# Three edits between the second feed-forward net and linear attention: gate products, weight loads, and the hand-over of the channel copies

## The chip, the cores and the metric
The kernel runs on one core of a Trainium2 chip. The metric is the device time of one execution, in microseconds (us); lower is better. The five engines named here are TensorE (PE, matrix products and transpositions; PEld is its weight load), VectorE (DVE), ScalarE (ACT), GpSimd (POOL) and SyncE (SP, which here only issues DMAs). Each works through its own queue in order, and they meet at semaphores.

## The reference, cut to what matters
A two-layer decoder over 4 batches of 512 tokens with 256 channels (2,048 tokens, 16 tiles of 128). Six blocks follow one another, each closed by a layer norm over channels:

```python
x = _layernorm(x + L0_attn(x))             # a recurrence with decay, 16 heads
x = _layernorm(x + L0_xattn(x, ctx))       # ternary weights, 8-bit activations, ends in a feed-forward net
x = _layernorm(x + L0_ffn(x))              # 8 experts, top 2 for each token
x = _layernorm(x + L1_attn(x))             # linear attention
x = _layernorm(x + L1_xattn(x, ctx))       # cross-attention to 1601 keys
x = _layernorm(x + L1_ffn(x))              # two layers of windowed attention and gelu net
```

The change touches the end of the second block, the third, and the start of the fourth. The experts' block takes scores `x @ Wg` (256 by 8), picks two experts for each token, sends the normalised token through `relu(h @ W1 + b1) @ W2 + b2` of each, and adds both, weighted, to the token. Linear attention begins with `q` and `kv` products of the token's 256 channels with a 256 by 768 matrix, `phi(x) = elu(x) + 1` on q and k.

## The kernel before, in words
Tokens are held twice: `x_tok` with tokens on the partitions (norms, sums) and `x_ch` with channels on the partitions (right operand or left operand of the next products). A group is the four tiles of one batch. The step from `x_tok` to `x_ch` is a *turn* of a group: eight transpositions on TensorE (`turn_pe`, L237) into two PSUM banks, then a copy of one half by ScalarE (L1520) and of the other by VectorE (L1490).

**End of the second block** (`bitnet_ffn_pe`, L1382 on). An output loop over 16 tiles makes 8 products for each (L1408); VectorE adds them to `x_tok` (L1473), and after each four tiles takes the norm of the group (L209 to L217). After tiles 7, 11 and 15 TensorE turns groups 0, 1 and 2. Behind the loop stand the gate products (`gate_pe`, L1433: products of `x_ch` with the 256 by 8 gate matrix) of groups 0, 1 and 2, then the turn of group 3, then the gate products of group 3. A `settle` lets every engine wait for the last copies of group 3. VectorE begins the experts with statistics of all 16 tiles (L1732), then reads the scores.

**Experts** (`experts_*`). SP loads the weights of experts 0, 1 and 2 (two DMAs of 1 MB each, L1630 and L1631), stores the normalised tokens `hats` to DRAM (L1639), then loads experts 3 to 7, with the bias matrix `b2` (L1644) after expert 4. VectorE and TensorE work out which 256 token rows go to which of 23 slots. GpSimd gathers the rows of a slot from `hats` with two indirect DMAs (L1995), slots 0 and 1 ahead of all else, the others as their buffers come free. For each slot TensorE transposes the rows (L1688), makes four groups of first products (L1704) and, one slot later, the second products (L1717). VectorE adds `b2` (L1890), GpSimd scatters the rows (L2012). When all slots are through, SP reads the pairs back, VectorE combines them group by group (L1898), and each group is normed by ScalarE (L1973, which waits for a reciprocal and a mean of VectorE, L1919 and L1921) and turned by TensorE. ScalarE's order is: norm of group g, then copy of group g - 1. VectorE's is: combine group g, finish the norm scale of g - 1, copy group g - 2.

**Start of linear attention** (`linear_*`). A `settle` makes all engines but SP wait for the last copies of group 3; SP waits for them too after it has issued the loads of `wqkv` and `wproj`. TensorE then makes the q and kv products of batch 0 (L2186 two steps, L2193 four steps), of batch 1, and so on, each step into the next of banks 4 to 7. For a q step VectorE takes the minimum (L2255), ScalarE makes relu and exp, VectorE adds (L2257).

Of the kernel before, what the change touches and what calls it, by code (L numbers as in the profile page):

```python
# [14 lines left out]
B, T, D = 4, 512, 256  # L15
NTOK = B * T
TILES = NTOK // P
# [321 lines left out]

def settle(m, last, but=None):  # L340

    nc = m.nc
    for e in (nc.tensor, nc.vector, nc.scalar, nc.gpsimd, nc.sync):
        if e is but:
            continue
        for wait in last:
            e.wait_ge(*wait)
# [1033 lines left out]
def bitnet_ffn_pe(m, s, t, use):  # L1381
# [20 lines left out]
    for tile in range(TILES):  # L1402
# [7 lines left out]
        if tile % 4 == 3 and tile > 4:  # L1410
            g = tile // 4 - 1
            pe.wait_ge(*s.normed(TPB * g + TPB))
            for h in range(HALVES):
                turn_pe(m, use["channels", g, h], m.x_tok, g, h)
    for g in range(B - 1):
        gate_pe(m, s, t, use, g)
    pe.wait_ge(*s.normed(TILES))
# [136 lines left out]
def experts(m, gate, split):  # L1554
    nc = m.nc
    with ExitStack() as ctx:
# [39 lines left out]
        steps = [("place",), ("inverse",)] + [p for p in plan if p[0] in ("turn", "first", "second")]  # L1596
        steps += [("channels", g, h) for g in range(B) for h in range(HALVES)]
        use = m.banks(steps, tuple(range(8)))
        use["gate",] = gate
        experts_sp(m, s, moved, t, use, plan, split)  # L1600
        experts_pe(m, s, moved, t, use, plan)
        experts_dve(m, s, moved, t, use, plan)
        experts_act(m, s, t, use, plan)
        experts_pool(m, s, moved, t, use)
        over = [use["channels", B - 1, h].done for h in range(HALVES)]
        settle(m, over, but=nc.sync)
    return use["second", SLOTS - 1].full, over

# [5 lines left out]
def x_loaded(moved, j):  # L1614
    return (moved.x0_loaded, moved.x1_loaded)[j % 2]
# [10 lines left out]
def experts_sp(m, s, moved, t, use, plan, split):  # L1626
# [10 lines left out]
    for tile in range(0, TILES, 4):  # L1637
        sp.wait_ge(*s.hat_made(tile + 4))
        sp.dma_start(hats[:, tile:tile + 4, :], t["hat"][:, tile:tile + 4, :]).then_inc(*s.stored.up(16))  # L1639
    for e in range(3, NE):  # L1640
        weights(e)
        if e == 4:
            sp.wait_ge(*s.stored(16 * TILES // 4))
            sp.dma_start(t["b2"], dram["moe_b2"].unsqueeze(0).to_broadcast([P, NE, D])).then_inc(*s.b_loaded.up(16))  # L1644
# [9 lines left out]
def experts_pe(m, s, moved, t, use, plan):  # L1654
# [24 lines left out]
    for step in plan:  # L1679
# [27 lines left out]
        elif kind == "second":  # L1707
# [11 lines left out]
            ins.then_inc(*u.fill)  # L1719
    for g in range(B):  # L1720
        pe.wait_ge(*s.normed(TPB * g + TPB))
        for h in range(HALVES):
            turn_pe(m, use["channels", g, h], m.x_tok, g, h)


# [346 lines left out]

def linear_attention(m, kept, weights_free, over):
    nc = m.nc
    with ExitStack() as ctx:
# [12 lines left out]
                      "low raised phi v_copied scaled closed joined xw_loaded ctx_loaded k_stored0 k_stored1 w_high w_low c_split a_low b_low "  # L2088
                      "in_high v_ones x_high x_low q_high q_stored")
        plan = linear_plan()  # L2090
# [8 lines left out]
        use.update(m.banks([p for p in plan if p[0] in ("keys", "value", "queries")], (0, 2)))  # L2099
        linear_sp(m, s, t, use, plan, weights_free, over)  # L2100
        linear_pe(m, s, t, use, plan, nth)
        linear_dve(m, s, t, use, plan, nth)
        linear_act(m, s, t, use, plan, nth)
        linear_pool(m, s, t, plan, use)
        settle(m, [use["channels", B - 1, h].done for h in range(HALVES)] + [use["value", AHEAD - 1, KT - 1].done]
# [66 lines left out]

def linear_pe(m, s, t, use, plan, nth):
    pe = m.nc.tensor
    wqkv = t["wqkv"]
    loaded = (s.rg0_loaded, s.rg1_loaded, s.rg2_loaded, s.rg3_loaded)
    pe.wait_ge(*s.w_loaded(32))
    for step in plan:
        kind, b = step[:2] if len(step) > 1 else (step[0], None)
        if kind in PREPARED:  # L2180
            prepare_pe(m, s, t, use, step, 0)
        elif kind == "q":
            c, u = step[2], use[step]
            pe.wait_ge(*u.empty)
            for h in range(HALVES):
# [196 lines left out]

def linear_pool(m, s, t, plan, use):
    g = m.nc.gpsimd
    for n in range(AHEAD):
        g.memset(t["v"][n][:, :, :, NX:VC], 1.0).then_inc(*s.v_ones.up())
    g.wait_ge(*s.v_ones.now())
    for step in plan:
        kind, b = step[:2] if len(step) > 1 else (step[0], None)
        if kind == "parts":  # L2390
            g.wait_ge(*s.closed.now())
            g.wait_ge(*s.x_low.now())
            context_pool(m, s, t, b)
        elif kind == "x_split":
            split_pool(m, s, t, use, b)
        elif kind == "scale":
            g.wait_ge(*s.scaled(b + 1))
            g.tensor_tensor(projected(m, b), projected(m, b), over_tiles(m, "la_beta"), ALU.add).then_inc(*s.closed.up())
# [1201 lines left out]
def build(nc, dram):  # L3600
# [8 lines left out]
    with ExitStack() as ctx:  # L3609
# [7 lines left out]
        with ExitStack() as first:  # L3617
# [7 lines left out]
            gate, split = bitnet(m, early)  # L3625
        weights_free, over = experts(m, gate, split)
        with ExitStack() as both:
# [4 lines left out]
                        c_high=[kb("xa_c_high%d" % n, [P, S2 + 1]) for n in range(2)], c_both=[kb("xa_c_both%d" % n, [P, S2 + 1]) for n in range(2)])  # L3632
            linear_attention(m, kept, weights_free, over)
            cross_attention(m, kept)
# [61 lines left out]
```

## Time and profile before
| | us |
|---|---|
| three runs, median (lowest to highest) | 2683.3 (2679.48 to 2683.9) |
| the profiled execution, its own time | 2684.69 |
| its span | 2683.4 |
| TensorE busy in the span | 2180.8 (81%) |
| VectorE busy | 1690.6 (63%) |
| ScalarE busy | 1192.3 (44%) |
| GpSimd busy | 593.5 (22%) |

Engine busy times overlap, so they don't add up. The mean granted TensorE clock is 0.902 of 2.4 GHz. A row of the timeline gives the start in us, the time it covers, the engine, the line, the operation with its output and inputs, how many were merged, and in brackets the idle time of the engine before them and who ended it.

### The profile page before, as it was taken

Reading aid. Unit: us, or ns where it says so; the run is one execution under the profiler, and the core shown is the slowest. Engines: PE = TensorE matmul, PEld = TensorE weight load, DVE = VectorE, ACT = ScalarE, POOL = GpSimd, SP = SyncE. Lnnn points to the kernel's source line nnn. Section 1 sums busy time; section 2 is a strip of 40 time slices with the busy share of each in tenths; the row PEclk is TensorE's granted clock in tenths of the full one; section 3 lists DMA queues with packets and bytes.
Section 4 is the critical chain, followed back from the end, with each engine's and each line's share of the span. In section 5 each row is a group of like instructions: output and inputs, shape, how many; then the busy total and the mean of one; then the engine's idle time right before and its main releaser. Section 6 shows DMA issues by size and latency. Waiting matters only on the chain. (4 is left out here: it accounts for less than half of the span.)

```text
span 2683.4 us, 42293 instructions
## 1 busy us (share of the span) xinstructions
PE 2180.8 (81%) x15608; PEld 1421.8 (53%) x15678; DVE 1690.6 (63%) x3439; ACT 1192.3 (44%) x2208; POOL 593.5 (22%) x529
## 2 busy tenths in 40 slices
PE   5996689897659995877799999967887786888677
PEld 3554157575449994443255555543555443555444
DVE  4875965466866665666666666616776533777663
ACT  2123855454333332423155555545665433666442
POOL 2110013133036661012100000003221322222142
PEclk8997789898779996888799999987999897999899
DMA  4111024343071112332311111020000001000100
GB/s 140 47 47 47 0 64 143 125 126 95 34 289 49 49 51 99 93 82 81 81 26 38 26 25 38 14 93 2 1 1 1 11 1 62 1 1 1 43 9 24
DMA packets 98936, 144.74 MB, mean 54 GB/s; under 512 B 25052, under 2 KB 78768, under 8 KB 96176
## 3 DMA queue, kind: packets, MB, share of 16 engines
q1 hardware_dynamic: 94320, 129.97, 15.7%
q0 software_dynamic: 4416, 12.06, 1.5%
q8 instruction: 131, 2.15, 0.4%
q14 instruction: 69, 0.57, 0.1%
HBM read 102.08 MB, written 39.85 MB: 53 GB/s over the span
## 5 line engine op out<-in xcount | busy, mean ns | idle before, releaser
L2795 DVE TENSOR_REDUCE xa_max<-psum 128x1 f32<-128x1024 f32 (+1 forms) x256 | 248.5, 988 | 132.1 <-PE psum L2705 131.5
L2876 ACT ACTIVATE xa_work<-psum 128x1024 f32<-128x1024 f32 (+1 forms) x208 | 212.7, 1024 | 188.1 <-PE psum L2728 186.1
L2743 PE MATMUL psum<-xa_work,xa_values 128*33 128x128 f32 (+1 forms) x3328 | 224.0, 277 | 0.0
L2743 PEld LDWEIGHTS psum<-xa_work,xa_values 128*33 128x33 f32 (+1 forms) x3328 | 168.2, 111 | 73.7 <-issue 70.2
L3066 PE MATMUL psum<-wqkv_l,x_hl_l 128*128 128x512 bf16 x538 | 138.5, 404 | 65.7 <-POOL x_hl_l L3326 32.9
L3432 PE MATMUL psum<-h_ch_f,w_f 128*128 128x512 bf16 (+1 forms) x556 | 135.0, 397 | 34.3 <-issue 13.1
L995 POOL TENSOR_TENSOR text_q<-text_q 128x512 bf16<-128x512 f32 x64 | 80.7, 1275 | 345.9 <-ACT text_q L1365 345.7
L2728 PE MATMUL psum<-xa_query_rows,xa_key_rows 98*128 98x512 bf16 (+1 forms) x416 | 127.3, 388 | 8.4 <-ACT xa_work L2876 7.7
L1704 PE MATMUL psum<-moe_rows,moe_w 128*128 128x256 bf16 x1104 | 129.7, 275 | 5.0 <-issue 5.0
L2705 PE MATMUL psum<-xa_key_rows,xa_query_rows 96*128 96x512 bf16 (+1 forms) x512 | 126.6, 344 | 8.4 <-ACT xa_work L2876 3.7
L1960 ACT CAST x_ch<-moe_raw 128x512 bf16<-128x512 f32 x92 | 56.9, 618 | 158.3 <-DVE moe_raw L1875 157.7
L3066 PEld LDWEIGHTS psum<-wqkv_l,x_hl_l 128*128 128x128 bf16 x576 | 56.4, 103 | 132.0 <-issue 50.6
L1717 PE MATMUL psum<-moe_w,x_ch 128*128 x1104 | 124.1, 273 | 0.0
L3300 ACT ACTIVATE w_p_l<-psum,w_max_l 128x256 f32<-128x256 f32 (+1 forms) x256 | 110.4, 457 | 28.8 <-DVE w_max_l L3204 28.7
L1704 PEld LDWEIGHTS psum<-moe_rows,moe_w 128*128 x1104 | 108.8, 99 | 18.7 <-issue 5.6
L3432 PEld LDWEIGHTS psum<-h_ch_f,w_f 128*128 128x128 bf16 (+1 forms) x576 | 56.4, 102 | 110.2 <-issue 32.0
L1717 PEld LDWEIGHTS psum<-moe_w,x_ch 128*128 128x128 bf16 x1104 | 108.0, 98 | 12.5
L1236 PE MATMUL psum<-ctx_f,query_sum 128*128 128x512 f32 (+1 forms) x256 | 105.0, 536 | 7.9 <-DVE query_sum L1288 7.9
L3337 POOL TENSOR_TENSOR qk_other_l<-qk_raw_l,rotary_l 128x256 f32<-128x256 f32 x64 | 64.6, 1010 | 195.2 <-DVE qk_rot_l L3188 195.2
L1257 PE MATMUL psum<-ctx_f,probs_t_bn 128*128 128x128 f32 (+1 forms) x832 | 100.0, 277 | 2.8 <-DVE probs_t_bn L1314 2.7
L1358 ACT ACTIVATE probs_bn<-psum,softmax_bn 128x1024 f32<-128x1024 f32 x64 | 58.8, 924 | 90.7 <-DVE softmax_bn L1305 90.7
L1257 PEld LDWEIGHTS psum<-ctx_f,probs_t_bn 128*128 128x128 f32 (+1 forms) x832 | 95.4, 192 | 3.5 <-DVE probs_t_bn L1314 3.4
(474 smaller groups left out, 4851.0 us busy)
## 6 DMA issues: line engine op xcount, KB each, us to landing
text_q<-in_moe_w SPq DMA_DIRECT2D x64, 256.0 KB, 3.8
experts<-text_q SPq DMA_DIRECT2D x64, 256.0 KB, 3.0
moe_w<-experts SPq DMA_DIRECT2D x16, 1024.0 KB, 10.0
xa_key_rows<-cross_keys SPq DMA_DIRECT2D x48, 200.1 KB, 3.5
ctx_chunk<-in_ctxT SPq DMA_DIRECT2D x24, 300.0 KB, 3.1
cross_keys<-xa_k_hl SPq DMA_DIRECT2D x6, 800.5 KB, 3.8
moe_w<-pairs_out SPq DMA_DIRECT2D x8, 512.0 KB, 6.8
xa_ctx_f<-in_ctxT SPq DMA_DIRECT2D x4, 800.5 KB, 4.8
```

The costliest lines, as they stand in the source:

```text
L1236: ins = pe.matmul(u.wide[:, c0 - a:c1 - a], t["qsum"][:, n * P:(n + 1) * P], t["keys"][:, b * S2 + c0:b * S2 + c1], start=True, stop=True)
L1257: ins = pe.matmul(u.ap[:, 0:P], t["turned"][n % 2][0:rows, kt, :], t["values"][0:rows, n // TPB, kt, :], start=(kt == 0), stop=(kt == KT - 1))
L1704: ins = pe.matmul(u.ap[:, a * SLOT:(a + 1) * SLOT], w1[:, w, h, cf], t["x"][j % 2][:, x, h, :], start=(h, k) == (0, 0), stop=(h, k) == (1, 2))
L1717: ins = pe.matmul(u.ap[:, a * D:(a + 1) * D], t["hidden"][j % 2][:, x, f, q], w2[:, w, f, :], start=(f, k) == (0, 0), stop=(f, k) == (7, 2))
L2705: ins = pe.matmul(u.wide[:, x - c0:y - c0], t["q_rows"][n % 3][0:SPLIT, a, qt * P:(qt + 1) * P], t["k_rows"][n % 3][0:SPLIT, a, x:y], star ...
L2728: ins = pe.matmul(u.wide[0:rows, a * T:(a + 1) * T], t["k_rows"][n % 3][:, a, kt * P:kt * P + rows], t["q_rows"][n % 3][:, a, :], start=Tr ...
L2743: ins = pe.matmul(total.ap[a * LANE:a * LANE + VC, c:c + PIECE], t["v"][b][0:rows, kt, first + a, :], exps[0:rows, a, c:c + PIECE], start= ...
L2795: v.tensor_reduce(t["maxes"][n % 2][:, qt * HU + a, part:part + 1], u.wide[:, 0:c1 - c0], AX.X, ALU.max).then_inc(*u.free)
L2876: act.activation(t["exps"][k % EXPS][0:rows], u.wide[0:rows].rearrange("p (m q) -> p m q", q=T), ACT.Exp, scale=1.0 / float(np.sqrt(np.flo ...
L3066: ins = pe.matmul(b.ap, x[:, i, h, w * P:(w + 1) * P], t["wqkv"][:, j, h, cols], start=(h, n) == (0, 0), stop=(h, n) == (1, 2))
L3300: ins = act.activation(t["p"][n % 2][:, i, lo:2 * P], scores[:, i, :], ACT.Exp, bias=t["peak"][n % 2][:, i:i + 1], scale=8.0, accum_out=t[ ...
L3432: ins = pe.matmul(u.ap[0:rows, :], t["w1"][:, y, h, o:o + rows], t["h_ch"][g % 2][:, x, h, :], start=(h, n) == (0, 0), stop=(h, n) == (1, 2))
```

## The change
Three edits:

1. In the output loop of the second block, the gate products of group g - 1 follow the turn of group g (for g = 1 and 2). Behind the loop only the gate products of group 2 stand ahead of the turn of group 3.
2. SP waits until both gathers of slot 0 have landed before it loads experts 3 to 7. `b2` follows expert 3 rather than expert 4, and its own wait for the stored `hats` goes.
3. The `settle` between experts and linear attention goes. The turns of the four groups are a function that linear attention calls on TensorE: group 0 first, then the wait for `wqkv`, the first four steps of the plan (q, q, kv, kv of batch 0), then the turns of groups 1, 2 and 3, then the rest of the plan. Each q step waits for the copies of its batch. GpSimd and SP wait for the copies of group 3 as before; ScalarE and VectorE go on after their own last copy. The turns use banks 0 to 3; linear attention has semaphores of its own.

```diff
@@ bitnet_ffn_pe
             for h in range(HALVES):
                 turn_pe(m, use["channels", g, h], m.x_tok, g, h)
-    for g in range(B - 1):
-        gate_pe(m, s, t, use, g)
+            if g:
+                gate_pe(m, s, t, use, g - 1)
+    gate_pe(m, s, t, use, B - 2)
@@ experts
-        steps += [("channels", g, h) for g in range(B) for h in range(HALVES)]
         use = m.banks(steps, tuple(range(8)))
+        use.update(m.banks([("channels", g, h) for g in range(B) for h in range(HALVES)], tuple(range(4))))
-        experts_pe(m, s, moved, t, use, plan)
+        turn = experts_pe(m, s, moved, t, use, plan)
...
-        over = [use["channels", B - 1, h].done for h in range(HALVES)]
-        settle(m, over, but=nc.sync)
@@ experts_sp
+    sp.wait_ge(*x_loaded(moved, 0)(32))
     for e in range(3, NE):
         weights(e)
-        if e == 4:
-            sp.wait_ge(*s.stored(16 * TILES // 4))
+        if e == 3:
             sp.dma_start(t["b2"], ...)
@@ experts_pe
-    for g in range(B):
+    def turn(g):
         pe.wait_ge(*s.normed(TPB * g + TPB))
         for h in range(HALVES):
             turn_pe(m, use["channels", g, h], m.x_tok, g, h)
+    return turn
@@ linear_pe
+    turn(0)
     pe.wait_ge(*s.w_loaded(32))
-    for step in plan:
+    for n, step in enumerate(plan):
+        if n == 4:
+            for g in range(1, B):
+                turn(g)
...
         elif kind == "q":
+            for wait in channels[b]:
+                pe.wait_ge(*wait)
@@ linear_pool
+    for wait in over:
+        g.wait_ge(*wait)
```

## Rows read from the trace of the kernel before
**Rows 1.** Timeline, end of the second block: start, us covered, engine, line, operation.
```profile
714.04 3.66 PE L1408 MATMUL psum<-bn_q_f,hidden_q 128*128 128x256 bf16 x32
...
718.53 1.66 DVE L1473 SCALAR_TENSOR_TENSOR x_tok<-psum,out_scale,x_tok 128x256 f32<-128x256 f32 x4
719.16 1.06 PE L237 MATMUL psum<-const,x_tok 128*128 128x128 f32 x8 [1.46 <-DVE x_tok L1473]
...
720.06 8.29 PE L1433 MATMUL psum<-moe_wg,x_ch 128*128 128x8 f32 x48
...
723.25 1.38 DVE L217 TENSOR_SCALAR x_tok<-x_tok,ln_mean_var,ln_rstd 128x256 f32<-128x256 f32 x4
...
728.20 1.95 PE L237 MATMUL psum<-const,x_tok 128*128 128x128 f32 x8
...
730.19 0.69 DVE L1490 COPY x_ch<-psum 128x512 f32<-128x512 f32 x1 [5.55 <-PE psum L237]
...
731.03 3.55 PE L1433 MATMUL psum<-moe_wg,x_ch 128*128 128x8 f32 x16 [0.88 <-DVE x_ch L1490]
...
731.13 5.26 DVE L1732 BATCH_NORM_STATS2 ln_stats<-x_tok 128x6 f32<-128x256 f32 x16
```
**Rows 2.** Windows: us, busy (instructions) by engine, granted clock, DMA share, GB/s.
```profile
720.00:722.00 2.00, 2.00 (x22) 2.00 (x19) 1.93 (x6) 0.41 (x1) 0.00 (x0) 1.00 0.00 0
...
722.00:723.00 1.00, 1.00 (x8) 1.00 (x7) 0.64 (x5) 0.29 (x1) 0.00 (x0) 0.60 0.00 0
```
**Rows 3.** Timeline, the gathers of slots 0 and 2 and the first bias addition.
```profile
762.27 0.99 POOL L1995 DMA_INDIRECT moe_rows<-hats,come_from  x1 [0.30 <-issue]
...
768.71 1.12 PE L1688 MATMUL psum<-const,moe_rows 128*128 128x128 f32 x4 [9.20 <-DMA moe_rows<-hats,come_from]
...
780.15 0.95 POOL L1995 DMA_INDIRECT moe_rows<-hats,come_from  x1 [0.30 <-issue]
...
786.11 0.66 PE L1688 MATMUL psum<-const,moe_rows 128*128 128x128 f32 x4 [0.84 <-DMA moe_rows<-hats,come_from]
...
795.43 0.69 DVE L1890 TENSOR_TENSOR moe_rows<-psum,moe_rows 128x512 f32<-128x512 f32 x1
```
**Rows 4.** Line L1995 alone: issue to landing of all 46 gathers.
```profile
DMA to landing us min/median/max: 2.7/3.0/7.2
```
**Rows 5.** Waits in the experts' stretch: us in total, times, longest.
```profile
PEld psum L1688 <- DMA moe_rows<-hats,come_from: 10.5, 2, 9.4
```
**Rows 6.** Windows of the experts' start; last three numbers: clock, DMA share, GB/s.
```profile
764.00:766.00 2.00, 0.00 (x0) 0.00 (x0) 0.00 (x0) 0.00 (x0) 1.46 (x2) 0.50 1.01 414
...
793.00:800.00 7.00, 7.00 (x66) 6.32 (x65) 4.03 (x9) 2.68 (x5) 3.14 (x3) 1.00 0.12 41
```
**Rows 7.** Timeline, last norms of the experts and start of linear attention.
```profile
1056.89 0.56 ACT L1520 COPY x_ch<-psum 128x512 f32<-128x512 f32 x1
...
1064.10 2.07 ACT L1973 ACTIVATE x_tok<-x_tok,minus_mean,ln_rstd 128x256 f32<-128x256 f32 x4 [0.44 <-DVE minus_mean L1921]
...
1066.22 1.97 PE L237 MATMUL psum<-const,x_tok 128*128 128x128 f32 x8 [1.21 <-ACT x_tok L1973]
...
1068.23 0.69 DVE L1490 COPY x_ch<-psum 128x512 f32<-128x512 f32 x1 [2.49 <-PE psum L237]
...
1069.02 6.03 PE L2186 MATMUL psum<-x_ch,la_wqkv 128*128 128x512 f32 x8 [0.83 <-issue]
...
1072.81 0.75 DVE L2255 TENSOR_SCALAR la_min<-psum,cols 128x512 f32<-128x512 f32 x1 [3.65 <-PE psum L2186]
...
1074.89 7.03 PE L2193 MATMUL psum<-la_wqkv,x_ch 128*128 128x512 f32 x16
...
1079.57 0.68 DVE L2264 TENSOR_TENSOR la_kv<-psum,rows 128x512 f32<-128x512 f32 x1
...
1081.41 0.68 DVE L2264 TENSOR_TENSOR la_kv<-psum,rows 128x512 f32<-128x512 f32 x1
```
**Rows 8.** Windows, the clock at the start of linear attention (columns as in rows 2).
```profile
1073.00:1074.00 1.00, 1.00 (x2) 0.34 (x1) 0.56 (x1) 0.32 (x1) 0.00 (x0) 0.61 0.38 93
```

More of the change, by code:

```diff
@@ L337, in rwkv, with settle @@
         settle(m, last)
-def settle(m, last, but=None):
+def settle(m, last):
     nc = m.nc
     for e in (nc.tensor, nc.vector, nc.scalar, nc.gpsimd, nc.sync):
-        if e is but:
-            continue
         for wait in last:
@@ L1604, in experts @@
         experts_pool(m, s, moved, t, use)
-        over = [use["channels", B - 1, h].done for h in range(HALVES)]
-        settle(m, over, but=nc.sync)
-    return use["second", SLOTS - 1].full, over
+    return use["second", SLOTS - 1].full, turn, [[use["channels", g, h].done for h in range(HALVES)] for g in range(B)]
 def loaded(s, e):
@@ L2070, in value_steps, with linear_attention @@
     return [("value", b, kt) for kt in range(0, KT, 2)]
-def linear_attention(m, kept, weights_free, over):
+def linear_attention(m, kept, weights_free, turn, channels):
     nc = m.nc
@@ L2088, in linear_attention @@
                       "low raised phi v_copied scaled closed joined xw_loaded ctx_loaded k_stored0 k_stored1 w_high w_low c_split a_low b_low "
-                      "in_high v_ones x_high x_low q_high q_stored")
+                      "in_high v_ones x_high x_low q_high q_stored", first=80)
         plan = linear_plan()
@@ L2099, in linear_attention @@
         use.update(m.banks([p for p in plan if p[0] in ("keys", "value", "queries")], (0, 2)))
-        linear_sp(m, s, t, use, plan, weights_free, over)
-        linear_pe(m, s, t, use, plan, nth)
+        linear_sp(m, s, t, use, plan, weights_free, channels[B - 1])
+        linear_pe(m, s, t, use, plan, nth, turn, channels)
         linear_dve(m, s, t, use, plan, nth)
         linear_act(m, s, t, use, plan, nth)
-        linear_pool(m, s, t, plan, use)
+        linear_pool(m, s, t, plan, use, channels[B - 1])
         settle(m, [use["channels", B - 1, h].done for h in range(HALVES)] + [use["value", AHEAD - 1, KT - 1].done]
@@ L2170, in rows_sp, with linear_pe @@
     sp.dma_start(dram["cross_keys"][b].rearrange("x (o p) s -> o p x s", p=P)[o], t["k_hl"][o]).then_inc(*keys_stored(s, o).up(16))
-def linear_pe(m, s, t, use, plan, nth):
+def linear_pe(m, s, t, use, plan, nth, turn, channels):
     pe = m.nc.tensor
@@ L2380, in linear_act, with linear_pool @@
             bitnet_channels_act(m, use, b)
-def linear_pool(m, s, t, plan, use):
+def linear_pool(m, s, t, plan, use, over):
     g = m.nc.gpsimd
+    for wait in over:
+        g.wait_ge(*wait)
     for n in range(AHEAD):
@@ L3625, in build @@
             gate, split = bitnet(m, early)
-        weights_free, over = experts(m, gate, split)
+        weights_free, turn, channels = experts(m, gate, split)
         with ExitStack() as both:
@@ L3632, in build @@
                         c_high=[kb("xa_c_high%d" % n, [P, S2 + 1]) for n in range(2)], c_both=[kb("xa_c_both%d" % n, [P, S2 + 1]) for n in range(2)])
-            linear_attention(m, kept, weights_free, over)
+            linear_attention(m, kept, weights_free, turn, channels)
             cross_attention(m, kept)
```

## The prediction, made before the change was run
> **What bounds the kernel now.** I read the page first. Its first part has TensorE busy 81% of the span (the table above), but the three edits touch three short stretches in which it waits or works on something that nobody needs yet, so the share of the whole says nothing. I went on with the timeline of each stretch, asking each time which wait ends last, and with the windows for the granted clock and the DMA share.
>
> *End of the second block.* VectorE ends the norm of group 3 at 723.25 + 1.38 = 724.63, but TensorE turns the group only at 728.20, because 48 gate products stand in its queue until 728.35 [rows 1]. VectorE copies the turned half at 730.19 and starts the experts' statistics at 731.13. These end at 736.39; the last gate products end at 734.58, under them [rows 1]. So the statistics set the pace, and they hang on the turn.
>
> *Start of the experts.* TensorE waits 9.2 us for the gather of slot 0, issued at 762.27 and used at 768.71: 6.4 us, where the median of 46 gathers is 3.0 [rows 3, 4]. The DMA engines are full then (share 1.01), and nearly idle at 793 to 800, where TensorE is busy without a gap at full clock (share 0.12, busy 7.00 of 7.00) [rows 6]. Only one later gather is waited for [rows 5]: that of slot 2, issued 780.15, used 786.11, also about 6 us [rows 3]. What is saved ahead of slot 0 is thus kept to the end of the experts.
>
> *Start of linear attention.* After its last copy (1068.23 to 1068.92) VectorE stands idle 3.65 us until the first q product is there at 1072.81; TensorE starts at 1069.02 at half clock, and reaches 2.4 GHz at 1073.8 (0.61 in the window from 1073) [rows 7, 8]. From then on VectorE and ScalarE pass q and kv to and fro and TensorE is ahead.
>
> **Edit 1, gate products into the loop.** Nothing is added or removed: 48 products of 8 columns before, 16 + 16 + 16 after. At full clock 22 instructions fill 2.00 us [rows 2], so 16 cost 1.45 us. The 16 of group 0 now stand ahead of tiles 12 to 15, which take 3.66 us and end at 717.7; they would end at 719.2 [rows 1]. VectorE takes the four tiles from 718.53 at 0.41 us each, so it asks for the last at 719.8, and is not held up. The turn of group 2 starts at 719.25 for 719.16, 0.1 us late, and VectorE's chain with it: its norm of group 3 ends at 724.7. Meanwhile TensorE makes the gate products of group 1 (from 720.4) and 2 (to 723.4, if the clock holds; to about 724 if it falls at 722.6 as it does before, window 722 to 723 at 0.60 [rows 2]). Either way it is free, and turns group 3 at about 724.9 instead of 728.20. Price: **-3.3 us**. The last products are covered by the statistics with 736.39 - 734.58 = 1.8 us to spare. Bounds: if this turn also ran at full clock it would take 1.06 instead of 1.95 us [rows 1], so -4.2. At worst the clock falls while the gate products of group 0 run in the loop: these then take 2.9 us, the four tiles about 5.2 (half clock until the clock is back), the turn of group 2 starts at 722.3 and takes 1.95, and from its end VectorE needs the same 4.4 us (719.16 + 1.06 to 724.63) to the norm's end, 728.7: **+0.6**. I take the first: before, the clock fell 2.5 us into the gate products (720.06 to 722.6), and in the loop they last 1.45 us and output products follow at once.
>
> **Edit 2, weights held.** SP's ten loads of 1 MB and `b2` move behind the landing of slot 0's gathers. With idle queues I give the gather the median, 3.0 us: 762.27 + 3.0 = 765.3 for 768.71, **-3.4 us**. That the whole wait behind is engine work (transposition, cast, first products) makes it pass on. Queued behind SP's new wait: experts 3 to 7 and `b2`. At 414 GB/s [rows 6] these 11.5 MB take 28 us, 765 to 793. `b2`, third in the new order, has landed by some 773 and is first used at 795.43 - 3.4 = 792 [rows 3], so nearly 20 us are spare; expert 3, ahead of it in the queue, is used later still, in the fourth of 23 slots. The gather of slot 2 falls in the same crowd as before and I leave it its 6 us. Bounds: **0** if the first gather is slow for a reason of its own; if the gather of slot 2 comes with it, up to 0.84 us more [rows 3], -4.2; if that one takes the longest 7.2 us [rows 4] instead of 6.0, 1.2 is given back.
>
> Beside this the Trainium skill has a rule that speaks against the size of this term. "DMA: Bandwidth & Descriptors", section "Queues, rings and completion order", says that each DMA engine goes round between the queues that have work, one packet at a time, so a gather would not sit behind the backlog of the weights' queue but share with it. By that rule 256 KB beside a stream of 414 GB/s would lose about 0.6 us, an estimate, and not 3.4. The trace doesn't side with it: the two gathers that had a full stream beside them took twice the median. By the row the edit is worth 3.4, by the rule 0.6.
>
> **Edit 3, no stop.** The gain to be had is VectorE's 3.65 us of idling [rows 7]. But the turns of groups 1 to 3 now stand behind 16 fp32 products, and ScalarE copies group 1 before it norms group 3. On the clock of the trace before: copies of group 0 are done at 1056.89 + 0.56 = 1057.45, products start at 1057.5. At 1.2 GHz one takes 0.88, at 2.4 GHz 0.44 (7.03 / 16) [rows 7]. If the clock again rises 4.8 us after the first product (1069.02 to 1073.8 [rows 7, 8]), 5.5 are done by 1062.3 and the other 10.5 take 4.6: the turn of group 1 starts at 1066.9. At full clock it takes 1.06. VectorE copies group 1 from 1068.0 to 1068.7, then makes reciprocal and mean, for which ScalarE waits 0.44; the norm of group 3 starts at 1069.1 and takes 2.07 [rows 7]; the turn of group 3 starts at 1071.25; VectorE's last copy runs 1072.35 to 1073.04; the first q step of VectorE starts at about 1073.3, for 1072.81. Price: **+0.5 us**, and TensorE's head start hides nothing more, since VectorE doesn't wait for it after the first q step. The loads that SP issues behind the last copy come some 4 us later; they are first read only when VectorE is through batch 1. Bounds: if nothing is late but the products, the whole **-3.65**; if the clock stays at 1.2 GHz, 16 products take 14.1, turns 1.97, and VectorE starts at about 1079.8: **+7.0**.
>
> **Sum.** -3.3 - 3.4 + 0.5 = -6.2 us. Against the profiled execution's own 2684.69 us that is 2678.5. This execution lies 1.4 us over the median of the runs shown, 2683.3, so the median after should be 2683.3 - 6.2 = **2677.1**. No change is what lies within 0.2% (5.4 us) of the median, about what a measurement of this kernel can tell. The forecast stands just beyond that.
>
> **Rivals.**
> *The stop was worth its idle time* (edit 3 gives -3.65). For it: the 3.65 us are there. Against: group 3's norm waits behind ScalarE's copy of group 1, and that behind 16 products. Time: 2683.3 - 3.3 - 3.4 - 3.6 = 2673.0. Chance 0.12.
> *The first gather is slow by itself* (edit 2 gives 0): it is the first one after `hats` was written. Against: the gather of slot 2 was slow too. Time: 2683.3 - 3.3 + 0.5 = 2680.5. Chance 0.15. (The rule of the Trainium skill above, of "DMA: Bandwidth & Descriptors", would give near it, 2679.9.)
> *The clock falls inside the output loop* (edit 1 gives +0.6). For it: 8-column products now stand right behind a turn for which TensorE had idled, as they did where it fell. Time: 2683.3 + 0.6 - 3.4 + 0.5 = 2681.0. Chance 0.13.
> *Slower: TensorE stays at 1.2 GHz from 1057 to the end of batch 1's products.* It starts cold, is fed in pieces and is stopped three times by turns. Edit 3 then costs 7.0, and the kv steps of batch 1 come at 3.5 us each on TensorE while VectorE takes one in 1.84 (1079.57 to 1081.41 [rows 7]): over four steps at 1.7 us each, less the 2 us that TensorE is ahead, some 5 us more. Sum -6.7 + 12 = +5.3: 2688.6. It decides from the point where edit 3 costs over 6.7, which is where the turn of group 1 starts later than about 1071. Against: with 16 products in a row the clock rose after 4.8 us before. Chance 0.10.
>
> **How the numbers follow.** The forecast has 0.50. Its own scatter of some 2 us puts 0.31 of it beyond 5.4 us and 0.19 within. Faster: 0.31 + 0.12 + 0.02 = 0.45. Same: 0.19 + 0.15 + 0.11 less what scatters out = 0.42. Slower: the last rival and the scatter of the middle ones, 0.13. The range goes from 2672, the bound of the full gain of edit 3 and a little, to 2686, which takes in the middle rivals and the first 7 us of the slow one, and leaves out most of its rest.
>
> **What would show it.** Edit 1: the turn of group 3 within 0.5 us behind VectorE's norm of it, and tiles 12 to 15 read by VectorE without a gap. Edit 2: under 4 us from the issue of slot 0's second gather to TensorE's first transposition, with a DMA share near 0 in between. Edit 3: 16 products between the turns of groups 0 and 1; VectorE's first q step straight behind its last copy, its wait for the product gone; the time from ScalarE's copy of group 0 to that step 0.5 us longer than the 15.9 before (1056.89 to 1072.81 [rows 7]). I would be wrong if that stretch were shorter by over 2 us, if the gather stayed at 6, or if later stages, which the edits don't touch, moved by more than the sum.

## The result, and the profile after

The changed kernel takes 2671.21 us (median of 19 runs, 2666.8 to 2683.06), the kernel before beside it 2683.62 us (19 runs, 2679.48 to 2700.02). The ratio is 0.995, with a 95% interval from 0.9938 to 0.9962: 12.4 us faster, where I had forecast 6.2 and given a range that ended at 2672.0.

The page of the changed kernel, first part: busy time, share and instructions of each engine.
```profile
span 2681.7 us, 42368 instructions
...
PE 2188.0 (82%) x15678; PEld 1415.9 (53%) x15678; DVE 1691.5 (63%) x3439; ACT 1191.9 (44%) x2208; POOL 594.3 (22%) x529
```
Nothing was taken away; each engine is busy for the same time as before, to 0.5%. The execution that was profiled took 2683.06 us, the longest of the 19. Its first half is usual, its second half is not, so I read the second half from another profile of the same kernel (its own time 2671.95 us, below under "The changed kernel again").

**Edit 1.** Timeline of the changed kernel at the end of the second block; it answers to [rows 1]. Columns: start, us covered, engine, line, operation, idle before and releaser.
```profile
711.16 1.06 PE L237 MATMUL psum<-const,x_tok 128*128 128x128 f32 x8 [1.46 <-DVE x_tok L1472]
712.06 2.83 PE L1432 MATMUL psum<-moe_wg,x_ch 128*128 128x8 f32 x16
714.75 5.97 PE L1406 MATMUL psum<-bn_q_f,hidden_q 128*128 128x256 bf16 x32
...
718.36 0.48 DVE L1472 SCALAR_TENSOR_TENSOR x_tok<-psum,out_scale,x_tok 128x256 f32<-128x256 f32 x1 [1.22 <-PE psum L1406]
719.88 0.48 DVE L1472 SCALAR_TENSOR_TENSOR x_tok<-psum,out_scale,x_tok 128x256 f32<-128x256 f32 x1 [1.04 <-PE psum L1406]
720.56 1.04 PE L237 MATMUL psum<-const,x_tok 128*128 128x128 f32 x8
721.43 3.64 PE L1432 MATMUL psum<-moe_wg,x_ch 128*128 128x8 f32 x32
...
724.63 1.38 DVE L217 TENSOR_SCALAR x_tok<-x_tok,ln_mean_var,ln_rstd 128x256 f32<-128x256 f32 x4
726.06 1.73 PE L237 MATMUL psum<-const,x_tok 128*128 128x128 f32 x8 [0.99 <-DVE x_tok L217]
...
728.77 5.26 DVE L1732 BATCH_NORM_STATS2 ln_stats<-x_tok 128x6 f32<-128x256 f32 x16
```
The same kernel in windows: us, busy (instructions) of PE, PEld, DVE, ACT, POOL, granted clock, DMA share, GB/s.
```profile
712.06:713.00 0.94, 0.94 (x10) 0.94 (x9) 0.87 (x3) 0.35 (x1) 0.00 (x0) 0.84 0.00 0
713.00:714.75 1.75, 1.75 (x10) 1.75 (x11) 1.65 (x8) 0.03 (x1) 0.00 (x0) 0.50 0.00 0
714.75:717.00 2.25, 2.25 (x12) 1.61 (x13) 1.90 (x6) 0.26 (x1) 0.00 (x0) 0.50 0.00 0
717.00:720.50 3.50, 3.50 (x23) 2.64 (x21) 1.10 (x3) 0.00 (x0) 0.00 (x0) 0.64 0.00 0
```
The turn of group 3 starts 726.06 - 726.01 = 0.05 us behind VectorE's norm of it, as meant, and 3.6 us after the norm in the kernel before [rows 1]. But the clock falls to half, 1.2 GHz, during the gate products of group 0 and is still there in tiles 12 to 15: 16 gate products take 2.83 us and not 1.45, the four tiles 5.97 and not 3.66, VectorE stands waiting between the tiles, and the turn of group 2 comes 720.56 - 711.16 = 9.40 us after that of group 1, before 719.16 - 713.13 = 6.03. From the turn of group 1 to the statistics it is 17.61 us, before 18.00: **-0.4 us**.

**Edit 2.** Timeline of the changed kernel, the gathers of slots 0 and 2; it answers to [rows 3].
```profile
760.06 0.99 POOL L1995 DMA_INDIRECT moe_rows<-hats,come_from  x1 [0.30 <-issue]
762.91 1.11 PE L1685 MATMUL psum<-const,moe_rows 128*128 128x128 f32 x4 [5.66 <-DMA moe_rows<-hats,come_from]
774.35 0.95 POOL L1995 DMA_INDIRECT moe_rows<-hats,come_from  x1 [0.30 <-issue]
780.60 0.66 PE L1685 MATMUL psum<-const,moe_rows 128*128 128x128 f32 x4 [1.13 <-DMA moe_rows<-hats,come_from]
```
The window between the first two of them, columns as above.
```profile
760.06:762.91 2.85, 0.00 (x0) 0.00 (x0) 1.28 (x5) 0.00 (x0) 2.24 (x3) 0.58 0.32 92
```
From the issue of slot 0's second gather to the first transposition it is 2.85 us, before 6.44: **-3.6 us**. The DMA share is 0.32 instead of 1.01 [rows 6]. Slot 2's gather still takes 6.25 us.

**Edit 3.** Timeline of the changed kernel, start of linear attention; it answers to [rows 7].
```profile
1051.35 0.56 ACT L1519 COPY x_ch<-psum 128x512 f32<-128x512 f32 x1
...
1052.01 6.37 PE L2192 MATMUL psum<-x_ch,la_wqkv 128*128 128x512 f32 x8 [3.94 <-ACT x_ch L1519]
...
1058.22 3.60 PE L2199 MATMUL psum<-la_wqkv,x_ch 128*128 128x512 f32 x8
1061.65 1.91 PE L237 MATMUL psum<-const,x_tok 128*128 128x128 f32 x16
...
1063.73 2.07 ACT L1973 ACTIVATE x_tok<-x_tok,minus_mean,ln_rstd 128x256 f32<-128x256 f32 x4 [0.66 <-DVE minus_mean L1921]
1065.86 1.09 PE L237 MATMUL psum<-const,x_tok 128*128 128x128 f32 x8 [2.30 <-ACT x_tok L1973]
...
1066.99 0.69 DVE L1489 COPY x_ch<-psum 128x512 f32<-128x512 f32 x1 [2.69 <-PE psum L237]
1067.63 0.74 DVE L2261 TENSOR_SCALAR la_min<-psum,cols 128x512 f32<-128x512 f32 x1
```
The 16 products stand between the turns of groups 0 and 1, VectorE's first q step (L2261) follows its last copy without a wait, and from ScalarE's copy of group 0 to that step it is 1067.63 - 1051.35 = 16.28 us, before 15.92: **+0.4 us**. The 3.65 us of idling are gone, and the turns are that much later.

So the three edits, read where they stand, give -0.4 - 3.6 + 0.4 = -3.6 us in this execution. The measured gain of the medians is 12.4. The rest was sought by experiment.

### The profile page after: what moved, and what is told of

It is laid out like the page before. It is cut to its first block and busy times, and to the rows that moved or that the text cites. A ratio compares the mean times of both kernels' runs of the same rounds, so it can differ in the third digit from the quotient of the medians.

```text
span 2681.7 us, 42368 instructions
## 1 busy us (share of the span) xinstructions
PE 2188.0 (82%) x15678; PEld 1415.9 (53%) x15678; DVE 1691.5 (63%) x3439; ACT 1191.9 (44%) x2208; POOL 594.3 (22%) x529
## 5 line engine op out<-in xcount | busy, mean ns | idle before, releaser
L2751 PE MATMUL psum<-xa_work,xa_values 128*33 128x128 f32 (+1 forms) x3328 | 230.6, 283 | 0.0
L3074 PE MATMUL psum<-wqkv_l,x_hl_l 128*128 128x512 bf16 x576 | 145.9, 401 | 61.2 <-POOL x_hl_l L3334 32.4
```

The lines of the kernel that those rows point to most:

```text
L2751: ins = pe.matmul(total.ap[a * LANE:a * LANE + VC, c:c + PIECE], t["v"][b][0:rows, kt, first + a, :], exps[0:rows, a, c:c + PIECE], start= ...
L3074: ins = pe.matmul(b.ap, x[:, i, h, w * P:(w + 1) * P], t["wqkv"][:, j, h, cols], start=(h, n) == (0, 0), stop=(h, n) == (1, 2))
```

## A ruler for the whole kernel

To find where the rest comes from, every profile is cut at five places: TensorE's turn of group 1 (711.16 above), VectorE's first q step (1067.63), VectorE's cast of the identity at the start of cross-attention (`xa_ident_b`), its copy of `xa_parts_t`, and its first reciprocal of the last stage (`qk_norm_l`). The last three look like this in the kernel before.
```profile
1279.31 0.23 DVE L2786 CAST xa_ident_b<-const 128x128 bf16<-128x128 f32 x1 [1.69 <-DMA cross_queries<-xa_q_hl_l]
...
1324.50 0.40 DVE L2813 COPY xa_parts_t<-psum 4x512 bf16<-4x512 bf16 x1
...
1846.33 0.35 DVE L3173 RECIPROCAL qk_norm_l<-qk_norm_l 128x32 f32<-128x32 f32 x1
```
All profiles of the study (A: turn of group 1 to first q step, where all three edits lie; B: from there to the cast; C: cast to copy; D: copy to reciprocal; E: reciprocal to the end of the span; B to E hold no instruction that an edit touches, but for the first q and kv steps in B). "Measured" is the median, with that of the kernel before on the same chip.

| kernel | A | B | C | D | B+C+D | E | measured, before |
|---|---|---|---|---|---|---|---|
| before | 359.7 | 206.5 | 45.2 | 521.8 | **773.5** | 837.1 | 2683.6 |
| before again | 360.2 | 207.3 | 41.0 | 525.3 | **773.6** | 838.2 | 2683.4, 2682.9 |
| edit 1 | 359.4 | 206.2 | 42.6 | 525.2 | **774.0** | 841.6 | 2681.8, 2682.3 |
| edit 2 | 356.7 | 205.8 | 42.6 | 525.2 | **773.5** | 838.3 | 2680.2, 2682.3 |
| edit 3 | 360.5 | 204.3 | 39.4 | 522.2 | **765.8** | 837.5 | 2675.7, 2682.3 |
| edits 1 and 2 | 354.3 | 204.6 | 39.2 | 522.1 | **765.9** | 838.2 | 2670.4, 2682.3 |
| edits 2 and 3 | 357.2 | 204.8 | 39.3 | 522.1 | **766.3** | 838.8 | 2672.3, 2682.9 |
| all three (after) | 356.5 | 201.3 | 40.8 | 534.6 | 776.6 | 837.4 | 2671.2, 2683.6 |
| all three, again | 354.8 | 204.6 | 39.3 | 522.1 | **766.0** | 837.0 | 2668.5, 2681.4 |
| before + 5 copies | 361.7 | 204.0 | 39.2 | 522.1 | **765.3** | 836.4 | 2675.5, 2681.4 |
| before + 10 copies | 361.9 | 204.3 | 39.4 | 522.2 | **765.8** | 836.5 | 2677.3, 2681.4 |
| edit 2 + 5 copies | 357.5 | 205.4 | 39.2 | 522.1 | **766.6** | 838.2 | 2672.7, 2682.9 |
| all three + 5 copies | 356.5 | 206.4 | 39.2 | 522.2 | **767.9** | 841.7 | 2677.7, 2682.9 |
| edits 1 and 2 + 15 copies | 359.8 | 205.9 | 39.2 | 522.1 | **767.1** | 836.5 | 2674.4, 2681.4 |

Column A is what the edits do by themselves: against the mean of the two profiles of before (360.0) the change gives 3.5 and 5.1 us. It is good to 1 or 2 us only: 5 copies, which take 1.6 us, add 1.7 to it in one kernel and 0.8 in another, and 10 copies, which take 3.25, add 1.9. B+C+D has two values: 773.5 to 774.0 in four profiles, 765.3 to 767.9 in nine. The longest execution of the changed kernel, the one first profiled, stands outside both.

These are one profile for each row, and single executions of one kernel differ too. Of the 127 executions of the kernel before on record, 12 took less than 2676 us, as the short kernels do, and 11 more than 2692; most lie between 2680 and 2686. Long executions go with a lower mean granted clock: 0.911 for the shortest (2666.68 us), 0.894 for the longest (2703.40). So the two values are what most executions of a version do, not what its code must do.

## The experiments

Three theories were named; their letters have nothing to do with the columns. Theory A: the edits' local costs are all there is. Theory B: edit 3's order gives 6 us more inside linear attention. Theory C: the edits only shift the later stages against the granted clock, and these stages come out longer or shorter by that.

Each version ran 12 times (edits 1 and 2 together 6 times, edits 2 and 3 together 9), beside 29 to 35 executions of the kernel before. The ratio is not the quotient of the two medians, and for a difference this small the two can disagree; where the 95% interval takes in 1, the medians show no difference by themselves.

**Edit 1 alone** (before, and this):
```diff
                 turn_pe(m, use["channels", g, h], m.x_tok, g, h)
-    for g in range(B - 1):
-        gate_pe(m, s, t, use, g)
+            if g:
+                gate_pe(m, s, t, use, g - 1)
+    gate_pe(m, s, t, use, B - 2)
```


> Kernel before with edit 1 alone (gate products in the output loop). Theory A, each edit is worth its local term and nothing else: -0.4 us by the trace after, where the loop's clock fell and the stretch from the turn of group 1 to the first statistics went from 18.0 to 17.6 us; -3.3 if the clock holds. Theory B, the 6 us more than predicted come from edit 3's order in linear attention: the same, -0.4 to -3.3. Theory C, any shift of the work against the chip's clock changes what clock later stages get: the local term plus something between -8 and +8, seen in linear attention or cross-attention.

Measured: 2681.75 us for 2682.34, ratio 0.999 (0.9971 to 1.0009). In its profile the output products of tiles 12 to 15 took 6.26 us, and from the turn of group 1 to the statistics it is 726.16 - 708.81 = 17.35 us for 18.00:
```profile
708.81 1.06 PE L237 MATMUL psum<-const,x_tok 128*128 128x128 f32 x8 [1.46 <-DVE x_tok L1474]
...
712.12 6.26 PE L1408 MATMUL psum<-bn_q_f,hidden_q 128*128 128x256 bf16 x32
...
726.16 5.26 DVE L1733 BATCH_NORM_STATS2 ln_stats<-x_tok 128x6 f32<-128x256 f32 x16
```
With edits 1 and 2 it is 16.20 us, in the second profile of the changed kernel 728.97 - 712.75 = 16.22. Against the 18.00 of the first profile edit 1 is thus worth 0.4 to 1.8 us. The stretch varies without edit 1 as well: it is 17.94 in the second profile of before, and 17.33 to 18.58 in the other profiles in which its length can be read. So the value is rough, but in no profile is the stretch shorter than 16.19, and a gain of 3.3 us is not there.

**Edit 2 alone**:
```diff
+    sp.wait_ge(*x_loaded(moved, 0)(32))
     for e in range(3, NE):
         weights(e)
-        if e == 4:
-            sp.wait_ge(*s.stored(16 * TILES // 4))
+        if e == 3:
```


> Kernel before with edit 2 alone (weights of experts 3 to 7 behind the landing of slot 0's gathers). Theories A and B: -3.5 us, the wait for the first gather 2.9 instead of 6.4 us, all later starts earlier by that. Theory C: -3.5 and something more of either sign in the later stages.

Measured: 2680.22 for 2682.34, ratio 1.0003 (0.9982 to 1.0024; two of the 12 executions took 2697 and 2700 us). Locally it does the whole of what was forecast: 764.23 - 761.41 = 2.82 us for 6.44, and A is 3.4 us shorter.
```profile
761.41 0.99 POOL L1995 DMA_INDIRECT moe_rows<-hats,come_from  x1 [0.30 <-issue]
...
764.23 1.12 PE L1688 MATMUL psum<-const,moe_rows 128*128 128x128 f32 x4 [5.59 <-DMA moe_rows<-hats,come_from]
```
The gain is in the trace, but 3.4 us in 2680 are too little for this comparison to tell from nothing.

**Edit 3 alone** (the change without the hunks of edits 1 and 2):
```diff
+        if n == 4:
+            for g in range(1, B):
+                turn(g)
```


> Kernel before with edit 3 alone (turns of groups 1 to 3 behind four steps of linear attention, no stop). Theory A: +0.3 us. Theory B: -6 to -9 us, gained inside linear attention, between its first q step and the last norm. Theory C: +0.3 and something of either sign.

Measured: 2675.7 for 2682.34, ratio 0.9974 (0.996 to 0.9988). The stretch that edit 3 alters is 1069.35 - 1053.62 = 15.73 us for 15.92. Yet the kernel is 6.6 us faster, more than by the edit that saves 3.4. Alone this would have spoken for Theory B.

**Edits 1 and 2 together**, linear attention as before:


> Kernel before with edits 1 and 2 (the change without edit 3). Theory A: the sum of the two alone, -3.9 to -6.8. Theory B: the same, so the change as a whole is 6 to 9 faster than this kernel. Theory C: not the sum of the two alone.

Measured: 2670.4 for 2682.34, ratio 0.9958 (0.9943 to 0.9972). Without edit 3 nearly the whole gain is there, so Theory B is out. By the medians Theory A is out as well: edits 1 and 2 had -0.6 and -2.1 alone and have -11.9 together; the intervals of three kernels are wide, and the delays below decide it better. B+C+D is 765.9 with both and 774.0 and 773.5 with either.

**The changed kernel again**, unchanged, for a second profile:


> The kernel with the change, unaltered, run again beside the others and profiled again. Both theories: some 12 us faster than before. Theory C (where the clock falls in linear attention and cross-attention is another than before, and that is what the edits don't explain): its trace is ahead of the trace before by about 5 us at the start of linear attention, and by 8 or more us more at its end, with fewer stretches at half clock in between. Theory B (the order of edit 3): the same gain, but spread over the steps behind the turns and at the same clock.

Measured: 2668.5 for 2681.41, ratio 0.9948 (0.9929 to 0.9967). Against the second profile of before its span is 11.2 us shorter: A gives 5.4, B+C+D 7.6, E 1.2, and the stages ahead of the first edit, which are the same, take 3.0 back (the turn of group 1 at 712.75 for 709.76).

**Pure delays.** The kernel before, with 5 or 10 copies of 256 columns that nobody needs, on VectorE ahead of its last copy at the end of the experts. They do no work and lie on the path:
```diff
     bitnet_channels_dve(m, use, B - 2)
+    v.wait_ge(*use["channels", B - 1, 1].full)
+    for n in range(5):
+        v.tensor_copy(t["b2"][:, 1, :], t["b2"][:, 0, :]).then_inc(*s.v_step.up())
+        v.wait_ge(*s.v_step.now())
     bitnet_channels_dve(m, use, B - 1)
```


> The kernel before with 5 such copies, a pure delay of about 1.7 us ahead of linear attention. If nothing but the work counts: 1.7 us slower than before. Theory C: anything from 6 us faster to 6 us slower than before; faster than before at all would show that the moment at which a stage starts is worth more than the delay.

> The kernel before with 10 such copies, a delay of about 3.4 us at the same place. If nothing but the work counts: 3.4 us slower than before, and twice as much as with 5 copies. Theory C: not on one line with the run of 5 copies.

Measured: with 5 copies 2675.54 for 2681.41, ratio 0.998 (0.9965 to 0.9995); with 10, 2677.26, ratio 0.9991 (0.9977 to 1.0005), which by itself is no difference, though its B+C+D is short too. The copies are there and cost their time:
```profile
1066.42 1.60 DVE L1914 COPY moe_rows<-moe_rows 128x256 f32<-128x256 f32 x5 [2.49 <-PE psum L237]
1068.06 0.69 DVE L1490 COPY x_ch<-psum 128x512 f32<-128x512 f32 x1
...
1072.64 0.75 DVE L2259 TENSOR_SCALAR la_min<-psum,cols 128x512 f32<-128x512 f32 x1 [3.65 <-PE psum L2190]
```
A is 1.7 us longer, and B+C+D 8.2 us shorter. A kernel that only waits longer is 5.9 us faster by the medians, and 1.3 us at least by the interval, where Theory A has it 1.7 slower. Of the three theories only C allows this.

**Edits 1 and 2, 15 copies** (as above, `range(15)`), back to the start of the kernel before:


> Edits 1 and 2, and 15 small VectorE copies of the bias matrix (about 0.33 us each, 5 us in all) ahead of its copy of group 3's turned half, while every other engine waits: this puts back, just ahead of linear attention, the time that the two edits save. Theory C: the extra gain goes as well, and the kernel is within 2 us of the kernel before, about 2681 to 2683. If the extra gain belongs to the edits themselves and not to the moment at which linear attention starts: 5 us slower than edits 1 and 2 alone, about 2675.5.

Measured: 2674.41 for 2681.41, ratio 0.9976 (0.9962 to 0.999). A is 359.8, the same as before, yet B+C+D stays at 767.1. The expectation of Theory C, 2681 to 2683, was a miss; the other reading of that expectation, 5 us slower than edits 1 and 2 alone (2675.5), came within 1.1. How long A is does not by itself pick the outcome.

**The kernel before again**, unchanged:


> The kernel before once more, unchanged. Every theory: the same time as before, ratio 1.000. It is run for a second profile: Theory C says that the second part of linear attention, from the 1600th to the 1860th instruction of VectorE, is then again about 185 us long, and not 178; if it is 178 here, that part varies by itself and the seven microseconds are no property of the start.

Measured: 2683.43 for 2682.93, ratio 1.0002 (0.9981 to 1.0024). C is 41.0 here and 45.2 in the first profile, D 525.3 and 521.8; the sum B+C+D is 773.6 and 773.5. The part I had named (from the 1600th to the 1860th instruction of VectorE) was some 180 us here, between the 185 and the 178 of that expectation, so that part does vary by itself. The long value of the whole stretch came in both profiles of this kernel.

**Edit 2 and 5 copies.** The expectation places the copies wrongly: they stand at the end of the experts, as in the other delays.


> Edit 2 alone, and five small copies (1.7 us) on VectorE before the last turned half of the second block. Theory A (local costs alone): edit 2 gives 3.5, the copies cost 1.7, so 1.8 below before: 2680. Theory C (the start against the clock decides what clock the second part of linear attention gets): the start moves from a place where nothing was gained to one between it and before's, where pure delays gained; the second part is 178 us instead of 181 to 185 and cross-attention 525, the time 2673 to 2676.

Measured: 2672.72 for 2682.93, ratio 0.9966 (0.9952 to 0.998). Edit 2 alone had 2.1 us by the medians; with 1.6 us of copies it has 10.2. Windows from the cast to the copy (column C) and from the copy to the reciprocal (D), columns as above, edit 2 alone:
```profile
1274.50:1317.05 42.55, 37.33 (x156) 13.13 (x157) 28.91 (x37) 4.65 (x5) 11.58 (x7) 0.77 0.41 102
1317.05:1842.22 525.17, 476.07 (x4589) 281.05 (x4588) 295.68 (x456) 269.05 (x300) 25.10 (x22) 0.94 0.12 34
```
and with the copies:
```profile
1272.47:1311.65 39.18, 32.76 (x154) 12.49 (x157) 28.82 (x37) 4.65 (x5) 11.58 (x7) 0.87 0.44 111
1311.65:1833.70 522.05, 471.47 (x4586) 279.85 (x4588) 295.70 (x457) 269.04 (x300) 25.08 (x22) 0.94 0.12 35
```
In C these are the same instructions (157 weight loads, 37 on VectorE, 5 on ScalarE), the same bytes, and VectorE, ScalarE and GpSimd busy for the same time to 0.1 us. What differs is the granted clock, 0.77 against 0.87, and with it TensorE, busy 37.33 and 32.76 us. In time at full speed that was missing it is 42.55 x 0.23 = 9.8 us against 39.18 x 0.13 = 5.1. The waits in column C (us in total, times, longest) show it passed on, edit 2 alone:
```profile
ACT xa_work L2525 <- PE psum L2442: 21.1, 4, 9.3
...
DVE xa_work L2478 <- ACT xa_work L2525: 11.5, 4, 5.8
```
and with the copies:
```profile
ACT xa_work L2529 <- PE psum L2446: 17.2, 4, 8.2
...
DVE xa_work L2482 <- ACT xa_work L2529: 8.0, 3, 5.1
```
ScalarE waits 3.9 us less for TensorE's key products, VectorE 3.5 us less for ScalarE, and the stretch is 3.4 us shorter. In finer windows, edit 2 alone has the clock at 0.51 from 1284 to 1289, in the middle of these key products, where the kernel with the copies has 1.00:
```profile
1284.00:1289.00 5.00, 4.51 (x11) 1.09 (x11) 2.89 (x4) 0.00 (x0) 0.00 (x0) 0.51 1.07 239
```
with the copies:
```profile
1282.00:1287.00 5.00, 3.09 (x14) 1.04 (x14) 2.91 (x4) 1.11 (x1) 0.00 (x0) 1.00 1.07 253
```
Column D is 3.1 us shorter, and here the mean clock of the whole stretch (0.94 in both) is too coarse to show why. VectorE runs the same instructions in both kernels, and its distance behind the copy is the same to 0.2 us up to 375 us after it. Then edit 2 alone has ten microseconds at half clock:
```profile
1697.00:1707.00 10.00, 10.00 (x58) 4.49 (x56) 5.93 (x10) 4.22 (x6) 1.60 (x1) 0.51 0.00 1
```
The same place with the copies, 380 us behind the copy as well, has full clock, and TensorE gets through 98 products for 58:
```profile
1691.65:1701.65 10.00, 9.27 (x98) 5.62 (x96) 7.23 (x11) 6.76 (x9) 1.68 (x1) 1.00 0.00 1
```
VectorE's reciprocals of `ln_rstd` and `xa_rsum` on either side of this window are 1711.60 - 1697.14 = 14.46 us apart in the first, 1702.52 - 1691.86 = 10.66 in the second. These 3.8 us, of which 0.7 are won back behind, are D's difference. The two other profiles with D at 525 (edit 1 alone, and before again) have the clock at 0.50 in the same place; all with D at 522 have 0.99 or 1.00 there.

The odd first profile of the changed kernel is told by the same thing. Its D is 12.5 us longer than in the second profile, and it has stretches at half clock that the second lacks, among them this one:
```profile
1461.00:1470.00 9.00, 9.00 (x48) 4.02 (x48) 4.97 (x7) 3.46 (x5) 0.73 (x1) 0.50 0.00 0
```
The second profile has at the same place:
```profile
1462.75:1471.75 9.00, 8.27 (x80) 4.80 (x80) 6.24 (x9) 5.50 (x8) 1.28 (x1) 1.00 0.01 2
```

**Edits 2 and 3**, gate products behind the loop:


> Edits 2 and 3, gate products left behind the output loop. Theory A: 3.5 below before, about 2679. Theory C: at the end of the experts it stands 3 to 4 us ahead of before, as edit 2 alone does, so it may gain nothing in linear attention (2680), or take the good outcome (2671 to 2673); edit 1's share in the change is what it then lacks against after: 0.5 to 2 us.

Measured: 2672.29 for 2682.93, ratio 0.9964 (0.9946 to 0.9982). Short outcome. A is 357.2, with edit 1 added 356.5 and 354.8; that fits edit 1's share, 0.7 to 2.4 us.

**All three and 5 copies**:


> All three edits and the five small copies (1.7 us). Theory A: 1.7 slower than after, 2670.3. Theory C: either the same outcome, 1.7 slower, or the clock pattern with the loss, 2676 to 2678.

Measured: 2677.65 for 2682.93, ratio 0.998 (0.9971 to 0.9989), 5.3 us below before where the second run of the changed kernel was 12.9 below: 7.6 us lost. The copies cost 1.6. B+C+D is 1.9 us longer, and E 4.7 (841.7 for 837.0, as with edit 1 alone), where the last stage has a second value of its own: in these two profiles its mean clock is 0.91, in the others 0.92. No version run here is faster than the change beyond what the intervals leave open.

## Why the prediction was wrong

The direction was right, the size was not: 6.2 forecast, 12.4 measured.

*Edit 1, forecast -3.3, measured -0.4 to -1.8.* The turn of group 3 follows the norm as forecast. The step that failed is "in the loop they last 1.45 us and output products follow at once": I took the time that passed before the clock fell in the kernel before for a respite that the loop would have too. (I also misread it: a mean of 0.60 from 722 to 723 puts the fall at 722.2, so it was 2.1 us and not 2.5.) In the loop the clock fell 0.6 us after the first gate product in the first profile of the change, and 2.1 us after it, among the output products, in the second: the large products behind did not keep it up. The rival "the clock falls inside the output loop" was the true one; its parts were 2.9 and 5.2 us, found were 2.83 and 5.97 in one execution, 1.85 and 5.32 in another. Its price of +0.6 was too high, because it let the turn of group 2 run at half clock too (1.95 us); the clock was back by then, and that turn took 1.04:
```profile
713.65 1.85 PE L1432 MATMUL psum<-moe_wg,x_ch 128*128 128x8 f32 x16
...
715.36 5.32 PE L1406 MATMUL psum<-bn_q_f,hidden_q 128*128 128x256 bf16 x32
```

*Edit 2, forecast -3.4, measured -3.6.* Right in cause and size: in all eight profiles with edit 2 the gather takes 2.8 us to its first use, in the six without it 6.0 to 6.8. The estimate of 0.6 us, worked out from the Trainium skill's rule of turns between queues ("DMA: Bandwidth & Descriptors", "Queues, rings and completion order"), isn't what the rows show; whether the queues take turns in another way than the estimate has it, no run here tells. Where TensorE waited for slot 2's gather, it took 6.2 to 6.8 us with the edit and 5.9 to 6.4 without, about as expected.

*Edit 3, forecast +0.5, measured +0.4, 0.0 in the second profile, -0.2 with edit 3 alone.* Right within the scatter. TensorE's clock rose some 5.4 us after the first product (1052.01, and 0.18 x 3 us before 1058 by these windows of the changed kernel), where 4.8 were assumed:
```profile
1051.00:1055.00 4.00, 2.99 (x4) 1.46 (x5) 3.90 (x15) 1.11 (x3) 0.00 (x0) 0.50 0.00 0
1055.00:1058.00 3.00, 3.00 (x5) 1.18 (x5) 0.30 (x4) 2.07 (x4) 0.00 (x0) 0.59 0.00 0
1058.00:1062.00 4.00, 4.00 (x13) 1.82 (x12) 0.00 (x0) 0.00 (x0) 0.00 (x0) 1.00 0.00 0
```

*The sum.* Forecast -6.2, by column A -3.5 and -5.1. Had the rest of the kernel stood still, the median would have been 2683.6 less this, 2678.5 to 2680.1.

*The step that failed most* is one that the working never states: that a sum of local terms, made against one execution, is the difference of the medians. The stages behind, from the first q step to the last stage, had been 773.5 us long in the kernel before and are 766 in the changed one. This is 7.6 us of the 11.2 by which the second profiles of the two kernels differ, the largest term, and almost nothing of it is touched by an edit. The sum had put it at nothing. I had listed it among what would make me wrong (later stages that move by more than the sum) and given it no place in the range. Shown by experiment: the size of it (four profiles at 773.5 to 774.0, nine at 765.3 to 767.9), that a pure delay brings it as well as a gain does, and, for the 3.4 us of column C and the 3.1 of column D, that the granted clock of TensorE is what differs. For the 0 to 3 us by which column B differs this wasn't followed up. That the measured time lies below the range is thus no credit to the edits: they gave less than the forecast, and the stages behind gave the rest.

*Open.* Which start gives which outcome. The first q step stood at 1068.25, 1068.75, 1070.00 and 1072.81 in the long profiles and at 1069.35, 1071.23, 1071.58 and 1072.64 in short ones, between them. Neither this time nor column A picks the value. One thing does go with it. In every profile the clock falls within 2.1 us of VectorE's cast at the start of cross-attention; from 3.5 to 4.5 us after the cast it is back at 1.00 in all nine short profiles, and still at 0.50 in all four long ones. This says where the outcomes part, not why the clock comes back earlier or later. Each kernel had its outcome in its profile and in its median alike, save the one long execution of the changed kernel. The short one may therefore be good fortune of this version, and the next edit upstream may lose such a gain: five copies took 7.6 us of it back, though by B, the last stage and their own 1.6 us, and not by C and D.

## What to carry to other kernels

A local term of 3 us in a kernel of 2680 us can be right to 0.2 us, as edit 2's was, and still say little about the total, when later stages run in and out of half clock: their length can change with any edit ahead of them, one that only waits too. Give that a term of its own in the range (here 0 to -8 us for a kernel found in the long outcome), and test it with a harmless delay on the path: if waiting 1.6 us longer makes the kernel faster, a gain of that size measured for an edit need not be the edit's. Products of a few columns are not free to move into a loop of large ones; the loop may then run at half clock.

## What the hardware showed unexpectedly

- With sixteen products of 8 columns in the output loop, behind a turn for which TensorE had waited 1.46 us, the clock fell to 0.50 between 0.6 and 2.1 us after the first of them, as it had 2.1 us into the 48 of the kernel before [rows 2]; that large products followed at once did not prevent it. These 32 products took 5.0 to 6.3 us for 3.66.
- The same products of cross-attention met full clock in one kernel and ten microseconds of half clock in another (1.00 and 0.51 in the windows above), though the two differ only in five copies some 600 us earlier.
- With five copies of 0.32 us each added on VectorE a kernel of 2681.4 us was 5.9 us faster (ratio 0.998, 0.9965 to 0.9995).
- A gather issued under a full stream of loads took 6.0 to 6.8 us to its first use, and 2.8 us without it.
